# Cross attention in two layers on one core: the mask's bits in two rings, and the turned maxima sent by ScalarE

## The reference

```python
q = x @ Wq + bq;  k = ctx @ Wk + bk;  v = ctx @ Wv + bv
scores = einsum(q, k) / sqrt(16) + mask          # mask: 112 x 375 for each batch
attn = softmax(scores, axis=-1)
out = einsum(attn, v) @ Wo + bo
x = layernorm(out + x) * gamma + beta            # the input of the second layer
```

## Time and profile before

| | |
|---|---|
| median of three runs | 1731.52 us |
| the profiled execution's own time | 1728.31 us |
| its span, first to last instruction | 1726.5 us |
| PE busy | 1695.4 us, 98% |
| VectorE (DVE) busy | 1266.7 us, 73% |
| ScalarE (ACT) busy | 1041.5 us, 60% |
| GpSimd (POOL) busy | 572.2 us, 33% |
| mean granted clock of PE | 0.997 |

### The profile page before, as it was taken

How to read it: one execution, slowest core, us unless ns; L and a number is a source line. 1 busy time by engine, 2 the same in 40 slices (tenths; PEclk the granted TensorE clock), 3 DMA queues, 4 the chain that set the end, 5 groups by cost and what they waited for, 6 DMA issues and landing times. The chain is left out here.

```text
span 1726.5 us, 36049 instructions
## 1 busy us (share of the span) xinstructions
PE 1695.4 (98%) x10911; PEld 1007.9 (58%) x10911; DVE 1266.7 (73%) x1713; ACT 1041.5 (60%) x2370; POOL 572.2 (33%) x1169
## 2 busy tenths in 40 slices
PE   7999999999999999999999999999999999999997
PEld 4556556566556565565665565665665655656652
DVE  5578777777777787776787776777776877767776
ACT  2566666665666566665656665666665666656564
POOL 3133333233333333332333332333323333323332
PEclk9999999999999999999999999999999999999999
DMA  7656555546545555546565455455454455454541
GB/s 242 160 150 151 145 145 122 143 120 155 148 121 143 135 131 146 151 116 156 147 169 149 127 123 134 112 140 147 106 133 130 121 139 141 108 136 114 141 114 55
DMA packets 288534, 235.83 MB, mean 137 GB/s; under 512 B 140874, under 2 KB 262980, under 8 KB 288356
## 3 DMA queue, kind: packets, MB, share of 16 engines
q1 hardware_dynamic: 267524, 205.82, 45.6%
q10 hardware_dynamic: 20960, 29.38, 7.3%
HBM read 101.39 MB, written 22.02 MB: 71 GB/s over the span
## 5 line engine op out<-in xcount | busy, mean ns | idle before, releaser
L940 DVE TENSOR_REDUCE mx<-ms 128x2 f32<-128x750 f32 x896 | 809.4, 925 | 397.2 <-PE ms L1112 391.2
L765 ACT ACTIVATE probs<-sc 125x448 f32<-125x448 f32 x1522 | 744.0, 542 | 280.0 <-PE sc L1083 276.0
L1112 PE MATMUL ms<-ks,qs 96*128 96x375 bf16 (+1 forms) x2560 | 437.9, 324 | 12.4 <-DVE mx L940 9.3
L1083 PE MATMUL sc<-qs,ks 99*125 99x448 bf16 x1522 | 427.0, 357 | 1.8 <-ACT probs L765 1.5
L1133 PE MATMUL pv<-probs,vs 125*32 125x448 f32 x3048 | 312.8, 543 | 0.0
L1083 PEld LDWEIGHTS sc<-qs,ks 99*125 99x125 bf16 x1522 | 192.5, 136 | 198.4 <-ACT probs L765 126.2
L1112 PEld LDWEIGHTS ms<-ks,qs 96*128 96x128 bf16 (+1 forms) x2560 | 174.0, 98 | 190.8 <-issue 66.5
L1190 PE MATMUL job<-wo,on 128*112 128x512 f32 x504 | 257.3, 592 | 0.0
L956 DVE RECIPROCAL orec<-osum 128x112 f32<-128x112 f32 x256 | 213.2, 835 | 4.2 <-DMA osum<-oraw 4.2
L1208 PE MATMUL job<-xT,wq 128*128 128x224 f32 x1008 | 214.3, 356 | 1.3 <-DMA xT<-in_xT 1.3
L1208 PEld LDWEIGHTS job<-xT,wq 128*128 128x128 f32 x1008 | 187.1, 190 | 20.9 <-ACT qf L807 7.1
(11 more groups left out here) (72 smaller groups left out, 1053.6 us busy)
## 6 DMA issues: line engine op xcount, KB each, us to landing
ctxT<-in_ctxT SPq DMA_DIRECT2D x64, 750.0 KB, 4.9
qs<-qp SPq DMA_DIRECT2D x756, 56.0 KB, 2.5
ks<-kp SPq DMA_DIRECT2D x768, 46.9 KB, 3.0
osum<-oraw ACTq DMA_DIRECT2D x125, 112.0 KB, 2.9
oc<-oraw ACTq DMA_DIRECT2D x125, 112.0 KB, 4.0
mask<-in_mask SPq DMA_DIRECT2D x64, 164.1 KB, 5.6
xT<-in_xT SPq DMA_DIRECT2D x32, 224.0 KB, 4.8
xin<-in_x SPq DMA_DIRECT2D x32, 224.0 KB, 3.1
```

The source lines that it names most:

```text
L765: nc.scalar.activation(probs[0:KCS, k, j, :], bank[0:KCS, 0:GL], ACT.Exp)\
L940: nc.vector.tensor_reduce(mx[o][:, cols], ms[n % 2][:, :, 0:S2], AX_X, ALU.max).then_inc(max_done[o], 1)
L1083: last = nc.tensor.matmul(bank[0:KCS, 0:GL], ks[p][0:KM, g, rows], qs[p][0:KM, g, :], start=True, stop=not masked)
L1112: last = nc.tensor.matmul(to, qs[o][0:KT, group, cols], ks[o][0:KT, group, :], start=True, stop=not masked)
```

## The change

Five things:

1. The DMA that writes the turned maxima into `qs` is issued by ACT within `m_out`, right behind the copy, with a wait for that copy; SP's `max_rows` and its calls are gone.
2. Of the seven loads of mask bits SP issues three (`BSYNC`), and ACT the other four, after its cast of the first keys.
3. Opening slots: the terms of parts 1 and 2 of `qs` for half 0 of unit 0 are issued by SP and not by ACT. In slot (1,-1) keys are projected at pieces 3 to 6 and not 0 to 3, GpSimd takes their parts after the maxima's, and ACT's cast of the key rests stands behind `m_out` at piece 7.
4. Layer 1's weights: the second half of Wq comes in two loads in two slots; Wo and the rows bo, gamma, beta come one slot later each.
5. `NW` counts the additional load.

```diff
-KEYS_AT = [{2: (0,), 3: (1, 2), 4: (3,)}, {2: (0, 1), 3: (2, 3)}, {0: (0,), 1: (1,), 2: (2,), 3: (3,)}]
+KEYS_AT = [{2: (0,), 3: (1, 2), 4: (3,)}, {2: (0, 1), 3: (2, 3)}, {3: (0,), 4: (1,), 5: (2,), 6: (3,)}]
...
-            def max_rows(p, h, value):
-                sp.wait_ge(mt_evac[p], value)
-                sp.dma_start(qs[p][KT:KM, 4 * h:4 * h + 4, :].rearrange("p g n -> p (g n)"), mT[:, :])\
-                  .then_inc(m_rows[p][h], 16)
...
             def opening_slot(p):
-                if p == 1:
-                    max_rows(0, 0, 1)
...
                     stack_terms(0, 0, qs[0], qp, 0, of=(0,))
+                    sp.wait_ge(q_p2[0], 2)
+                    stack_terms(0, 0, qs[0], qp, 0, of=(1,))
+                    sp.wait_ge(q_p3[0], 2)
+                    stack_terms(0, 0, qs[0], qp, 0, of=(2,))
                     stack_terms(0, 1, ks[0], kp[0], 1, of=(0,))
...
-                if m_ok:
-                    max_rows(p, 1, count(2 * main + 2))
...
-                if a_ok:
-                    max_rows(o, 0, count(2 * ahead + 1))
...
                 if (p, i) == (0, PER - 2):
-                    load_wq(1, w_in[1], slice(2, DC))
+                    load_wq(1, w_in[1], slice(2, 3))
                 if (p, i) == (1, PER - 2):
+                    load_wq(1, w_in[1], slice(3, DC))
+                if (p, i) == (0, PER - 1):
                     load_wo(1, rows_in[1], slice(0, 2))
-                if (p, i) == (0, PER - 1):
+                if (p, i) == (1, PER - 1):
                     load_wo(1, rows_in[1], slice(2, NG))
-                if (p, i) == (1, PER - 1):
+                if (p, i) == (0, PER):
                     for dst, key in ((bo, "bo"), (gamma, "gamma"), (beta, "beta")):
...
-            for n in range(BLOADS):
+            for n in range(BSYNC):
                 sp.dma_start(mbits[:, BROW * n:BROW * (n + 1)], mbits_d[n]).then_inc(mf_in[n], 16)
...
-                    key_rests()
                     max_parts(o, 0, ahead, None)
-                    key_lasts()
+                    key_parts()
...
                     nc.scalar.copy(mT[:, :], bank[0:PARTS * TILES, 0:P]).then_inc(mt_evac[u], 1)
+                    act.wait_ge(mt_evac[u], 2 * n + h + 1)
+                    act.dma_start(qs[u][KT:KM, 4 * h:4 * h + 4, :].rearrange("p g n -> p (g n)"), mT[:, :])\
+                       .then_inc(m_rows[u][h], 16)
...
                     cast_keys()
+                    for n in range(BSYNC, BLOADS):
+                        act.dma_start(mbits[:, BROW * n:BROW * (n + 1)], mbits_d[n]).then_inc(mf_in[n], 16)
...
-                    send(0, qs[0], qp, 0, (1,))
                     act.wait_ge(q_p3[0], 2)
-                    send(0, qs[0], qp, 0, (2,))
                     send(1, qs[0], qp, 0, (1, 2))
...
-                    if k == KEYS_END[q] + 1 and j_ok:
+                    if k == KEYS_END[q] + 1 and j_ok and not opens(p, i):
                         cast_keys()
...
+                    if opens(p, i) and k == COLUMNS_AT[q][0]:
+                        cast_keys()
```

More of the change, by code:

```diff
@@ L47 @@
 BLOADS = 7
+BSYNC = 3
 BROW = B * S * S2 // (BLOADS * P)
@@ L355, in cross_attention_two_layers @@
         yT_out = two(sem, "yT_out")
-        NK, NQ, NV, NW, NR = 2, 2, 2, (3, 7), (2, 5)
+        NK, NQ, NV, NW, NR = 2, 2, 2, (3, 8), (2, 5)
         block = ctx.enter_context(nc.Block())
@@ L459, in last_slots @@
                 if last_scores(p, i):
-                    max_rows(p, 1, 2 * main + 2)
                     outputs(0, 1, post, None)
```

## The result

The changed kernel takes 1785.99 us (median of 4 runs, 1784.93 to 1789.0) against 1729.97 for the kernel before (4 runs, 1727.7 to 1732.39). The ratio is 1.0325, 95% interval 1.0309 to 1.0341: a little over 3% slower. The forecast was 1788, between 1767 and 1806. The profiled execution took 1786.61 us, 58.3 more than that of before.

The account below looks back on a forecast made before the run. PE was taken as the bound, busy 1695.4 of 1726.5 us. Loop 59.0, opening -1, layer change -0.9 and end +1 made +58 on 1728.31, so 1786.3 (1789.6 from the median); given as 1788, range 1767 to 1806.

Parts of the forecast that it names:

- An issue on ACT holds up the next exp: Steady loop: ACT's next exp waits until the DMA issue ends, 0.77 us, and starts 0.10 later.
- The wait on the own copy: Steady loop, ACT: waiting for its own copy before the issue adds some 0.04 us.
- copy + 1.17: Steady loop: the next exp pair starts 1.17 us after the copy's start (0.26 + 0.04 + 0.77 + 0.10), today 0.19.
- The rule for PE: A score pair ends 0.54 us after its start or 0.45 after the exp pair freeing its banks, whichever is later.
- The four places: PE's delay per copy: p=0 piece 8, 0.98 us; p=1 piece 7, 0.80; p=1 piece 2, 0.09; p=0 piece 3, 0.
- Sum of the loop: 128 copies over the slots: 32x0.98 + 31x0.80 + 31x0.09 = 59.0 us slower.
- Opening, -1: Opening slots: split bit loads, later keys and sends together give -1 us, between -4 and +4.
- Layer change, -0.9: Layer 1's weights: PE's 0.90 us context wait behind their loads goes, -0.9 us, between -1 and +1.
- hidden in part: Rival: half the issue on ACT is covered, some 0.4 us less at 63 places, +33, about 1763 us; chance 0.08.
- longer: Rival: ACT's ring holds oc and osum, so the issue takes 1.0 us or more, +81, about 1809 us; chance 0.08.
- faster: Rival: SP's queue is scarce and ACT's issue costs PE nothing, some 6 us saved, 1725 us; chance 0.05.
- no change: Rival: a PE wait lying behind makes good PE's delay, 1731 us; chance 0.04.

Follow-up runs that it names:

- e1: The changed kernel with SyncE issuing the transfer of the turned maxima again at its four old places: 1730.46 us, ratio 1.0002.
- e2: The kernel before with one edit, ACT issuing the transfer of the turned maxima right behind its copy: 1788.08 us, ratio 1.0328.
- e3: The kernel before with ACT issuing the transfer, and waiting for the copy, behind the exp pair of the next piece: 1738.37 us, ratio 1.0051.
- e4: The kernel before with ACT only waiting for its own copy, SyncE still issuing the transfer: 1736.48 us, ratio 1.0032.
- e6: The kernel before with the mask's bits in two rings (SyncE three loads, ACT four) as the only edit: 1732.04 us, ratio 1.0007.
- e9: The changed kernel with the issue behind the next piece's exp pair, but right behind the copy in the opening slot: 1734.41 us, ratio 1.0021.
- e5: e2 plus a second transfer of the same tile into a spare place in HBM, issued behind the first: 1844.63 us, ratio 1.0661.
- e10: The kernel before with ACT issuing only half 1's transfers, right behind the copy; half 0's stay with SyncE: 1731.64 us, ratio 1.0003.
- e7: The kernel before with only the later keys in slot (1,-1), with GpSimd's order and ACT's cast of key rests: 1729.07 us, ratio 0.9991.
- e11: The kernel before with the later keys of the opening and the new order of layer 1's weights: 1729.67 us, ratio 0.9988.
- e8: The kernel before with the new order of layer 1's weights alone: 1729.59 us, ratio 0.9997.

## Why the prediction was right

- **What bounds the kernel**: right. PE's time in the loop, paid once a round; e1 and e2 put the whole loss into it.
- **An issue on ACT holds up the next exp, and takes 0.77**: right (a median of 0.781; the exp 0.05 to 0.12 behind its end). It holds up what stands behind it, not what stands in front (e3).
- **The wait on the own copy, 0.04**: right for the issue, which starts 0.03 behind the copy's end, too small for an exp, which in e4 starts 0.12 behind it (0.19 later than in the overlapped order). The chain's copy + 1.17 came out as + 1.11 to + 1.21.
- **The rule for PE (a pair ends 0.45 after its exp pair)**: 0.45 or 0.46 at all three places.
- **The four places**: 0.98, 0.80, 0.09 and 0 predicted, 0.99, 0.74, 0.06 and 0.00 measured. The second was too large by the 0.06 by which that exp starts earlier than copy + 1.17.
- **Sum of the loop**: 59.0 predicted, and 1 for the end. Thirty rounds took 54.5, of which 1.2 belong to the context wait, and the last slots 2.2: 55.5 for what was put at 60.0, too high by 4.5 us. Some 2.4 of these are the 0.08 a round by which the four places were put too high (1.87 for 1.79), the rest is the count of the ends.
- **Opening, -1**: wrong sign, and the bits in two rings alone gained nothing that shows (e6); the opening was +1.5 in the profiled execution, inside the bounds. 1.07 of it is a loss that repeats in e9 and belongs to the later keys and to the issue, about half each; the other 0.46 is within the spread of equal openings (-1.2 to +1.7). The sends behind the new issue, which the prediction named, cost more in e2, where the keys are early.
- **Layer change, -0.9**: wrong sign, +1.2; not settled.
- **Rivals**: "hidden in part" fails on e5 and on the rows of after; "longer" on the median of 0.781; "faster" on the result, and its ground on e1 and e2: relieving SP's queue gained nothing; "no change" on the round.

The mechanism was right, but that the total met the profiled execution so closely (1786.3 forecast, 1786.61 measured) was luck: the loop's excess of 4.5 us cancelled with the two small terms of the wrong sign (-1.9 forecast, +2.7 measured). The 1788 that was given lies 2 us above the median.

## What to carry to other kernels

A DMA issue on a computing engine is, in this kernel, an instruction of about 0.5 to 0.8 us in that engine's order (up to 1.6 in the opening), and the instruction behind it pays, whether or not the datapath is idle. Before one is moved there, read for each place how long after it the bounding engine needs the next result, and put the issue behind the last instruction that this engine waits for, where it then runs beside it (e3, e9) or where other work of the bounding engine covers it (e10). A queue engine that waits much, like SP here with 98 us, isn't a bottleneck while nobody waits for what stands behind.

## What the runs showed of the hardware that was not expected

**Issues of the same tile take different times.** The same tile of 42 x 128 costs 0.78 us to issue into three rows of SBUF and 0.46 us into 42 rows in HBM (e5), and oc's issue has a median of 0.62. That points to the form of the transfer, but place may have a part: `osum` and `oc` have the same shape, and `osum`'s issue, which comes first, has a median of 0.48. Neither the two sides of the transfer nor the place was tried by itself.

**The clock makes part of the scatter.** In the last slots PE waits now and then (1.05 us for the maxima at 1687.3 in the kernel before, 1.01 at the same place in e1, 1.04 in e7), and in some traces its clock is then granted at less than full, in others not. PE in one stretch, in the kernel before and in e1 (stretch, length, busy, count, then the granted clock as a share of 2.4 GHz, DMA share, GB/s):

```profile
1688.00:1692.00 4.00, 3.81 (x39) 1.00 0.06 22
```

```profile
1688.00:1692.00 4.00, 3.56 (x16) 0.50 0.32 95
```

At 0.50, the 1.2 GHz level, e1 did 16 matmuls there. The stretch at 0.50 is 6.8 us long in e1 and e11, and 3.4 in e4, e6, e7 and e8. At half speed that should cost half of it, 3.4 and 1.7 us, and the distances to before rise by 2.9 (e1), 3.1 (e11) and 1.6 (the four others) between the copies around it, and by nothing in the change, e2, e3, e9 and e10, whose clock is 1.00 there (e5 has two low stretches in its last slots, and steps of 2.9 and 3.1). Right behind the wait the same 24 matmuls of the values take 4.07 us in e7 and 2.46 in the kernel before:

```profile
1684.97 4.07 PE L1134 MATMUL pv<-probs,vs 125*32 125x448 f32 x24
```

e5, where PE waits more in the loop, has two such stretches there, of 3.4 us each (near 1309 and 1421 us), and two of its rounds are 57.3 us long and not 55.8. The executions of one kernel go the same way: of the 82 of the kernel before in the three batches, the 27 with a mean granted clock of 0.997 took 1728.3 us on average, the 34 with 0.996 took 1731.1, and the 21 with 0.995 or 0.994 took 1733.0. It isn't the only source: in e4 and e9 the time doesn't follow the clock, and the first copy moves by up to 2.9 us between executions with the same opening. A difference of 2 us between two kernels here can be nothing but this, and a trace shows whether it is.
